# A DLRM tower on one core: the program unrolled, batch blocks of 128, 128, 96, 96 and 64 samples, MLP features alternating between two PSUM banks and engines, a ring of 32 row buffers

## What is computed

```python
e = jnp.stack([tbl_0[ids[:, 0]], ..., tbl_31[ids[:, 31]]], axis=1)   # 512 x 32 x 256, f32
dots = jnp.einsum('bnd,bmd->bnm', e, e)                              # 32 x 32 per sample
z = dots[:, iu, ju]                                                  # 496 pairs i < j
h = jnp.concatenate([z, dense_ctx], axis=1)                          # 512 x 512
h = jnp.maximum(h @ W_top1 + b_top1, 0.0)                            # 512 -> 512
h = jnp.maximum(h @ W_top2 + b_top2, 0.0)                            # 512 -> 256
y = h @ W_top3                                                       # 256 -> 1
```

## Time and profile before

| | |
|---|---|
| median of 3 runs | 184.57 us (183.14 to 185.96) |
| span of the profiled execution | 182.8 us |
| PE busy, weight loads busy | 143.7 us (79%), 126.9 us (69%) |
| DVE, ACT busy | 60.9 us (33%), 59.4 us (33%) |
| POOL busy | 122.2 us (67%), 128 gathers of 950 ns |
| DMA | 19.64 MB, mean 107 GB/s |

### The profile page before, as it was taken

One profiled execution on the slowest core, in us unless ns is written; L12 is line 12 of the kernel. 1 busy time (PEld: TensorE's weight loads), 2 busy tenths in 40 slices (PEclk: granted clock), 3 DMA queues, 4 the chain that ended last, 5 costly groups with the idle time before them and its releaser, 6 DMA issues.

```text
span 182.8 us, 3140 instructions
## 1 busy us (share of the span) xinstructions
PE 143.7 (79%) x1104; PEld 126.9 (69%) x1104; DVE 60.9 (33%) x183; ACT 59.4 (33%) x185; POOL 122.2 (67%) x134
## 2 busy tenths in 40 slices
PE   0467669866699998777699997866899997775995
PEld 0155559655499997555599996655799995563993
DVE  0101614361411276161602267150502455356002
ACT  2011504442321345151411535151503615356010
POOL 4777777777777777778777777777777777760000
PEclk9999988999999999999999999999999999999699
DMA  0378964333334333333343333333333333330000
GB/s 15 112 213 266 291 222 118 101 101 115 99 109 116 95 109 113 92 110 111 90 115 106 95 115 104 97 115 101 100 114 97 105 109 97 109 108 11 0 0 0
DMA packets 8169, 19.64 MB, mean 107 GB/s; under 512 B 2369, under 2 KB 3009, under 8 KB 8162
## 3 DMA queue, kind: packets, MB, share of 16 engines
q0 software_dynamic: 6144, 16.79, 31.7%
q1 hardware_dynamic: 1874, 2.76, 4.5%
q10 hardware_dynamic: 144, 0.00, 0.0%
HBM read 19.53 MB, written 0.00 MB: 107 GB/s over the span
## 4 chain that ended last, share of the span: by engine, by line
PE 46%; POOL 27%; DMA 12%; issue 10%; ACT 2%; DVE 1%; ACTq 0%
POOL rows L160 27%; PE gram_ps L178 16%; PE act_ps L221 13%; DMA rows<-tables,idx 10%; PE xt_ps L171 8%; PE dve_ps L221 4%; PE act_ps L232 2%; PE dve_ps L232 2%; ACT z L121 2%; PE act_ps L240 1%; DMA ids_sb<-ids 1%; DVE z L121 1%; ACT xt L352 0%; ACT xt L373 0%; DVE h L322 0%
## 5 line engine op out<-in xcount | busy, mean ns | idle before, releaser
L160 POOL DMA_INDIRECT rows<-tables,idx x128 | 121.5, 950 | 40.4 <-issue 31.4
L171 PE MATMUL xt_ps<-ident,rows 128*128 128x128 f32 x256 | 49.8, 295 | 32.3 <-DMA rows<-tables,idx 32.0
L178 PE MATMUL gram_ps<-xt 128*128 128x128 f32 x512 | 70.8, 282 | 2.8 <-ACT xt L352 2.2
L178 PEld LDWEIGHTS gram_ps<-xt 128*128 128x128 f32 x512 | 64.0, 196 | 4.7 <-ACT xt L352 3.1
L171 PEld LDWEIGHTS xt_ps<-ident,rows 128*128 128x128 f32 x256 | 28.7, 145 | 45.6 <-DMA rows<-tables,idx 37.5
L288 DVE COPY xt<-xt_ps 128x512 f32<-128x512 f32 x32 | 22.1, 692 | 88.1 <-PE xt_ps L171 88.0
L121 ACT COPY z<-gram_ps 32x64 f32 (+5 forms) x136 | 34.9, 257 | 40.9 <-PE gram_ps L178 39.5
L121 DVE COPY z<-gram_ps 32x64 f32 (+5 forms) x136 | 34.6, 254 | 6.6 <-PE gram_ps L178 5.0
L352 ACT COPY xt<-xt_ps 128x512 f32<-128x512 f32 x31 | 18.1, 585 | 53.2 <-PE xt_ps L171 52.9
L221 PE MATMUL act_ps<-z,w_sb 128*128 (+1 forms) x192 | 23.9, 288 | 1.9 <-DVE z L121 1.9
L221 PEld LDWEIGHTS act_ps<-z,w_sb 128*128 128x128 f32 x192 | 23.2, 202 | 2.4 <-DVE z L121 2.1
(11 more groups left out here) (12 smaller groups left out, 5.4 us busy)
## 6 DMA issues: line engine op xcount, KB each, us to landing
rows<-tables,idx POOLq DMA_INDIRECT x128, 2.7
w_sb<-w SPq DMA_DIRECT2D x8, 256.0 KB, 3.9
w_sb<-w SPq DMA_DIRECT2D x1, 512.0 KB, 5.4
ids_sb<-ids SPq DMA_DIRECT2D x1, 64.5 KB, 1.9
z<-dense SPq DMA_DIRECT2D x1, 64.0 KB, 1.9
vec_sb<-vectors ACTq DMA_DIRECT2D x1, 4.0 KB, 2.1
y<-y_row SPq DMA_DIRECT2D x1, 2.0 KB
```

The source lines that it names most:

```text
L160: pool.indirect_dma_start(rows[:, g % STEP, :], None, tables, bass.IndirectOffsetOnAxis(idx[:, g:g + 1], 0)).then_inc(rows_landed[g % STEP ...
L171: last = nc.tensor.transpose(xt_ps[:, bank, place, P * k:P * (k + 1)], rows[:, n, P * k:P * (k + 1)], ident[:])
L178: last = nc.tensor.matmul(gram_ps[:, n // HALF, n % HALF, :], x, x, start=(k == 0), stop=(k == CHUNKS - 1))
```

## The change

The three loops are gone: `step`, `mlp_stages` and `Fori` are replaced by one loop in Python over 64 pairs, so that PE, DVE and ACT have straight programs with fixed addresses and fixed semaphore values. The transposes, copies and grams stand in the same order as before. The rest of the diff, cut:

```diff
-STEP = 16
-BLOCK_STEPS = 2
-BLOCK = BLOCK_STEPS * STEP * QUADS
+RING = 32
+OCTET = 8
+BLOCK_OCTETS = ((0, 4), (4, 8), (8, 11), (11, 14), (14, 16))
+BLOCKS = len(BLOCK_OCTETS)
+WIDEST = 4 * OCTET_COLS
...
-        rows = sb("rows", [P, STEP, DIM])
+        rows = sb("rows", [P, RING, DIM])
...
-        h1_ps = [act_ps[:, 0, :], act_ps[:, 1, :], act_ps[:, 2, :], dve_ps[:, 0, :]]
-        h2_ps = [act_ps[:, 3, :], dve_ps[:, 1, :]]
-        y_ps = act_ps[0:1, 0, :]
+        h1_ps = [act_ps[:, 0, :], dve_ps[:, 0, :], act_ps[:, 1, :], dve_ps[:, 1, :]]
+        h2_ps = [act_ps[:, 2, :], dve_ps[:, 2, :]]
+        y_ps = act_ps[0:1, 3, :]
...
+        def block_of_pair(stage_pair):
+            for b in range(BLOCKS - 1):
+                if stage_pair == OCTET_PAIRS * BLOCK_OCTETS[b][1] + 1:
+                    return b
+            return None
...
-                if g >= STEP:
-                    pool.wait_ge(transposed, g - STEP + 1)
+                if g >= RING:
+                    pool.wait_ge(transposed, g - RING + 1)
...
                 for m in features:
+                    if m >= 2:
+                        pe.wait_ge(h1_dve if m % 2 else h1_act, 2 * b + 1)
+                    elif m == 0 and b:
+                        pe.wait_ge(y_copied, b)
                     for s in range(SLOTS):
-                        last = nc.tensor.matmul(h1_ps[m], w1_sb[:, s, P * m:P * (m + 1)],
-                                                z[:, s, bass.ds(col, BLOCK)],
+                        last = nc.tensor.matmul(h1_ps[m][:, 0:n], w1_sb[:, s, P * m:P * (m + 1)],
+                                                z[:, s, col:col + n],
                                                 start=(s == 0), stop=(s == SLOTS - 1))
-                last.then_inc(h1_done, 1)
+                    last.then_inc(h1_done, 1)
...
-                return {1: first, 2: lambda: h1_part(col, [N1 - 1]),
-                        4: lambda: h2_all(b), 5: lambda: y_all(b)}
+            def mlp_at(pair):
+                for stage, ahead in ((h1_first, 0), (lambda b: h1_part(b, (2, 3)), 1), (h2_all, 3), (y_all, 4)):
+                    b = block_of_pair(pair - ahead)
+                    if b is not None:
+                        stage(b)
...
-            for lo, hi in ((0, STEP), (STEP, GROUPS)):
+            for lo, hi in ((0, OCTET), (OCTET, GROUPS)):
```

## The result

The changed kernel takes 194.62 us (193.53 to 194.91) against 184.61 us for the kernel before in the same session: a ratio of 1.056, 95% interval 1.051 to 1.061. I had forecast 187.2 us and a range of 182.5 to 189.2. It is slower, and by about four times as much as my sum said.

The account below looks back on a forecast made before the run. POOL's gather pace up to 162.4 us, then a serial tail of about 17 us, bound the kernel. 182.8 + 3.8 - 0.3 - 0.8 = 185.5, or 187.2 us on the median's scale (+1.4%); range 182.5 to 189.2.

Parts of the forecast that it names:

- POOL's pace bounds the batch, ring and first indices bring nothing: Gathers up to 162.4 us: POOL keeps 1.2535 us a step; ring of 32 and shorter first index addition are worth 0.
- A record costs 0.112 us at every width up to 128: PE's matmul records: the 128-column weight load sets the pace, so 64 or 96 columns cost 0.112 us too.
- Rival A: PE's records: columns set the pace, 0.056 us at 64 and 0.084 at 96, giving 180.6 us; chance 0.13.
- The fourth block makes PE 3.8 us late: Fourth block at iteration 57: too few pairs follow to work off its 84 records, so the end comes 3.8 us later.
- rival B: Fourth block: a stage held by its gate on ACT and DVE stalls PE 1 to 2 us, 188.2 to 189.2; chance 0.17.
- the queues on DVE and ACT: Near the fourth block: dots and copies queued on both engines have enough air before PE's grams, so nothing was added.
- Tail -0.3 us: Last block at 64 columns: wide records unchanged, but relu, third layer and last copy shorter, 0.2 to 0.4 us saved.
- the clock, -0.8 us: Before the last block: PE's clock fall cost 1.7 us before and could go either way; half was taken as saved.
- A smaller thing that I had at zero: Unrolled programs: less register work for PE, 0.1 to 0.3 us a block, worth 0 in the middle of the batch.

Follow-up runs that it names:

- e13: Changed kernel with 3 and 8 filler matmuls of the identity in PE's two last stalls, ahead of the last block: 186.08 us.
- e15: e14 plus the 3 and 8 filler matmuls in PE's two last stalls: 182.91 us, ratio 0.994 to the kernel before.
- e14: Changed kernel with four blocks of 128 samples and 16 early matmuls that move the instruction fetches: 184.44 us, ratio 1.005 to the kernel before.
- e1: Changed kernel with its last block of 64 samples computed on 128 columns, same instruction count: 188.02 us.
- e2: Changed kernel with its last block of 64 samples computed on 96 columns, same instruction count: 187.86 us.
- e3: Kernel before, its last block's first two layers on 64 columns (half the results left out): 190.59 us against 184.27, ratio 1.034.
- e4: Changed kernel with four blocks of 128 samples instead of five blocks: 186.16 us, ratio 1.012 to the kernel before.
- e12: Changed kernel with blocks of 128, 128, 64, 96, 96 samples, in a slow session: 251.81 us (kernel before 232.35).
- e16: Changed kernel with blocks of 128, 128, 64, 96, 96 samples, in another slow session: 252.5 us (kernel before 232.81).

## Why the prediction was wrong

- *POOL's pace bounds the batch, ring and first indices bring nothing:* right. The last gather is at 162.60 (162.43).
- *A record costs 0.112 us at every width up to 128:* right at full clock, 1.8 us per 16 records at 96 columns in the changed kernel and at 64 in e13. Rival A (the columns set the pace) is refuted. It is not right at the lower level, where they cost 0.213.
- *The fourth block makes PE 3.8 us late:* right. 3.65 us by the last transposes, 3.2 us in time (e13 against e15, which has four blocks and 128 columns at the end). No gate of rival B held PE: PE's timeline has no row with a wait between 151.6 and 169.2. What I had put at nothing for the queues on DVE and ACT is 0.21 us behind the last transposes.
- *Tail -0.3 us:* right, 0.27 us.
- **The step that failed is the clock, -0.8 us.** I took its fall as an event of fixed length: half a chance that it comes, and 1.7 us when it does, the price read from a last block that streams 128 columns. The fall came, in all four executions (mean clocks 0.938 to 0.951), and its length was another one with 64 columns behind it. About 75 of the 80 wide records of the last block ran at 0.213 instead of 0.112 us. From the first record of the last block to the end of the span that is 5.94 us more than before, although that stretch is 0.27 us shorter at equal clock: the term measured +6.2 us. With 3.65 for the lateness, 0.21 for the queue and -0.27 for the tail it gives 9.8 us, the difference of the two spans (192.6 - 182.8). The 1.7 us that I took for the fall before were nearly right (1.5 by e15 against e14). I had used the width only to ask what a record costs, and not whether the clock comes back under it. The place to stop at was my own result: if the load sets the pace, the array gets half as many columns in the same time at 64, so the earlier trace rows, which have 128 columns, could not price the fall for the changed kernel. e1, e2 and e3 show that they did not, and e13, without the fall, takes 186.08 us, inside my range.

A smaller thing that I had at zero is right only in the middle of the batch: the unrolled program fetches its instructions more often (9 packets of 16 KB in the trace, 4 before). Near the end one fetch went with 1.7 us (e4 against e14). In the changed kernel itself the last fetch before the end of the gathers lies between 154 and 155 us, and PE, already behind, does not wait there.

## What to carry to other kernels

Where weight loads set the pace, narrowing the moving operand saved next to nothing (0.27 us here); behind a stall in which the clock fell, the narrow block was paid at half clock to the end. Two things to try in such a place are a wider stream (6.6 us with 128 columns and 6.8 with 96 here, though 96 had the clock back late in e12 and e16) and dummy matmuls in the stall (8.5 us here, 1.5 us with full-width blocks). When a batch is cut into more blocks, count records, not samples: a block of 96 samples cost PE as much as one of 128, and what does not fit into the room left before the last data arrives is paid in full. That it would cost nothing further ahead is not shown. In an unrolled program look where the instruction fetches fall before judging a difference of 1%.

## What the runs showed of the hardware that I had not expected

- The same block of 64-column float32 matmuls ran at either level, whichever it was at: all its 8.94 us at the 2.4 GHz level in e13, and 16.9 us at the 1.2 GHz level behind a fall in e3 (16.0 in the changed kernel). With 96 and 128 columns the clock came back 3.4 us after the fall in e2 and e1, and with 96 after 6.8 us in e12 and e16.
- At the lower level a record with a load of 128 columns takes 0.213 us at 64 columns too. Twice the stream's 0.055 of full clock would be 0.11 (an estimate), so the load must have slowed down as well.
- One 16 KB instruction fetch went with a gather that landed 1.04 us late (e4), and with the fetch elsewhere the gather was on time (e14). Six of seven fetches in the changed kernel's trace have gathers beside them that took 3.3 to 3.9 us to land.
